# Moving the low halves of the gated products from GpSimd to VectorE, the product copies ahead of weight work on ScalarE, and the token sums and stored x halves of a fused attention and expert kernel

## What is computed

```python
x = x + xattn(layernorm(x), ctx_512, W_k, b_k, ln_gamma, ln_beta)   # softmax over normalised scores
# on layernorm(x):
gate = einsum('btd,edf->ebtf', x, Wg)      # experts 0 and 1: + x Ga Gb
up   = einsum('btd,edf->ebtf', x, Wu)      # experts 0 and 1: + x Ua Ub
mid  = silu(gate) * up
out  = einsum('ebtf,efd->ebtd', mid, Wd)   # experts 0 and 1: + mid Da Db
x = x + einsum('bte,ebtd->btd', weights, out)
```

## Time and profile before

| | us |
|---|---|
| median of 3 runs (range) | 1147.43 (1147.41 to 1148.15) |
| time of the profiled execution | 1149.48 |
| its span, first to last instruction | 1147.8 |
| TensorE busy in the span | 1070.2 (93%) |
| VectorE, ScalarE, GpSimd busy | 776.0, 440.6, 259.8 |

### The profile page before, as it was taken

One profiled execution on the slowest core, in us unless ns is written; L12 is line 12 of the kernel. 1 busy time (PEld: TensorE's weight loads), 2 busy tenths in 40 slices (PEclk: granted clock), 3 DMA queues, 4 the chain that ended last, 5 costly groups with the idle time before them and its releaser, 6 DMA issues.

```text
span 1147.8 us, 12310 instructions
## 1 busy us (share of the span) xinstructions
PE 1070.2 (93%) x4680; PEld 862.9 (75%) x4680; DVE 776.0 (68%) x1155; ACT 440.6 (38%) x634; POOL 259.8 (23%) x184
## 2 busy tenths in 40 slices
PE   6899999688999999999999969899999999999998
PEld 4787777466887878787877758677777878787777
DVE  6788795849486675749485692866757484857743
ACT  3454242343344344434343333443433342534430
POOL 2511144204030221304030210402213040403122
PEclk8899999889999999999999979999999999999999
DMA  8310002253132331414150205102111111211111
GB/s 295 120 46 1 1 15 84 57 176 128 37 116 68 97 105 56 147 55 129 37 181 22 73 18 202 56 19 74 37 56 55 55 38 37 73 36 57 37 38 74
DMA packets 85692, 86.35 MB, mean 75 GB/s; under 512 B 4096, under 2 KB 61568, under 8 KB 84864
## 3 DMA queue, kind: packets, MB, share of 16 engines
q1 hardware_dynamic: 85344, 85.49, 22.9%
q10 hardware_dynamic: 288, 0.07, 0.0%
HBM read 70.86 MB, written 14.68 MB: 75 GB/s over the span
## 4 chain that ended last, share of the span: by engine, by line
PE 55%; DVE 25%; issue 10%; ACT 6%; DMA 3%; SPq 0%; POOL 0%; DVEq 0%; ACTq 0%; POOLq 0%
PE tiles L1361 9%; PE tiles L1363 9%; PE tiles L1362 9%; PE gate_up L1471 6%; PE gate_up L1473 6%; PE gate_up L1472 6%; DVE mids L1131 5%; DVE wd_lo L1093 3%; ACT piece_hi L725 3%; DVE piece_lo L1085 2%; DVE piece L1073 2%; DVE piece L1074 2%; PE gate_up L1430 1%; PE gate_up L1429 1%; PE gate_up L1435 1%
## 5 line engine op out<-in xcount | busy, mean ns | idle before, releaser
L527 POOL TENSOR_TENSOR mids_lo<-mids,mids_hi 128x512 fp32r<-128x512 f32 x112 | 181.5, 1638 | 555.2 <-ACT mids_hi L759 554.6
L1471 PE MATMUL gate_up<-xT_hi,piece_hi 128*128 128x512 f32 x448 | 179.1, 400 | 29.8 <-ACT u_sb L745 28.1
L1085 DVE TENSOR_TENSOR piece_lo<-piece,piece_hi 128x1024 fp32r<-128x1024 f32 x112 | 133.7, 1235 | 106.0 <-ACT piece_hi L725 106.0
L1137 DVE SCALAR_TENSOR_TENSOR xacc<-tiles,rw,xacc 128x512 f32<-128x512 f32 x112 | 78.0, 750 | 163.0 <-PE tiles L1363 163.0
L1361 PE MATMUL tiles<-wd_hi,mids_hi 128*128 128x512 f32 x448 | 176.4, 394 | 9.6 <-POOL mids_lo L527 5.8
L1362 PE MATMUL tiles<-wd_lo,mids_hi 128*128 128x512 f32 x448 | 176.0, 393 | 0.0
L1363 PE MATMUL tiles<-wd_hi,mids_lo 128*128 128x512 f32 x448 | 175.9, 393 | 0.0
L1472 PE MATMUL gate_up<-xT_hi,piece_lo 128*128 128x512 f32 x448 | 175.9, 393 | 0.0
L1473 PE MATMUL gate_up<-xT_lo,piece_hi 128*128 128x512 f32 x448 | 175.4, 391 | 0.0
L1471 PE MATMUL gate_up<-tx_hi,piece_hi 128*128 128x512 f32 x336 | 133.9, 398 | 19.9 <-ACT s_sb L735 16.4
L1472 PE MATMUL gate_up<-tx_hi,piece_lo 128*128 128x512 f32 x336 | 132.3, 394 | 0.0
(11 more groups left out here) (165 smaller groups left out, 1559.6 us busy)
## 6 DMA issues: line engine op xcount, KB each, us to landing
piece<-in_wg_dram SPq DMA_DIRECT2D x40, 256.0 KB, 3.2
piece<-in_wu_dram SPq DMA_DIRECT2D x40, 256.0 KB, 3.3
wd_raw<-in_wd_dram SPq DMA_DIRECT2D x10, 1024.0 KB, 5.1
piece<-merged SPq DMA_DIRECT2D x32, 256.0 KB, 3.3
merged<-lora_w SPq DMA_DIRECT2D x6, 1024.0 KB, 5.3
w_raw<-in_xT_dram SPq DMA_DIRECT2D x4, 1024.0 KB, 6.1
wd_raw<-merged SPq DMA_DIRECT2D x4, 1024.0 KB, 5.6
out_dram<-xacc SPq DMA_DIRECT2D x16, 256.0 KB, 4.5
```

The source lines that it names most:

```text
L527: nc.gpsimd.tensor_tensor(mids_lo[h][:, f, :], mids[h][:, f, :], plain(mids_hi[h][:, f, :]), ALU.subtract)\
L1085: ins = nc.vector.tensor_tensor(piece_lo[j % 3][:, first:last, :], piece[j % 3][:, first:last, :], plain(piece_hi[j % 3][:, first - 1:last ...
L1137: nc.vector.scalar_tensor_tensor(tile_of(b, t), tiles[:, t, :], rw[:, (b * TT + t) * E + s:(b * TT + t) * E + s + 1], tile_of(b, t), ALU.m ...
L1471: nc.tensor.matmul(dst, w_h, x_h, start=first and kt == 0, stop=False, skip_group_check=True)
```

## The change

It moves `mid_low_part`, `lora_b_low_part` and `x_sum` from GpSimd to VectorE; writes VectorE's and ScalarE's orders anew, so that in a regular step the three product copies come before the weight pieces; forms the token sums for steps 0 to 6 between block 3's units; stores x of blocks 2 and 3 as its high and low halves straight from `xT_hi` and `xT_lo` (4 DMAs of 1 MB), loads three of the seven operands of step 7 back in place by six DMAs from GpSimd's queue (`load_again`), and forms the other four in `x_back` during step 6; issues the loads of pieces in step 0 ahead of the wait for the store of `xacc`; and gives the pieces' semaphores one instance per buffer.

```diff
-            sp.wait_ge(x_staged, TT)
-            sp.dma_start(x_spill[0, :, :], zt[:, :, :].rearrange("p t c -> p (t c)")).then_inc(x_stored, 16)
+            def store_x(a):
+                sp.wait_ge(xT_lo_ready, (a + 1) * TT)
+                for part, xT_part in enumerate((xT_hi, xT_lo)):
+                    sp.dma_start(x_spill[a - 2, part, :, :], plain(xT_part[:, a * KT * S:(a + 1) * KT * S])).then_inc(x_stored, 16)
+
+            def quadrant(b, part, first):
+                return x_spill[b, part, :, first * S:(first + 2) * S]
+
+            def load_back(slot, source):
+                sp.dma_start(x_back[:, slot, :], source).then_inc(x_back_loaded, 16)
+
+            store_x(B - 2)
...
+            store_x(B - 1)
...
             sp.dma_start(acc_spill, xacc[:, 2 * TT * D:]).then_inc(acc_stored, 16)
+            load_next_piece(3)
             sp.wait_ge(acc_stored, 16)
-            for k in range(STEPS):
+            load_lora(0)
+            load_next_piece(4)
+            load_next_piece(5)
+            store_merged(0)
+            for k in range(1, STEPS):
...
+                    load_back(0, quadrant(1, 0, 0))
+                    load_back(1, quadrant(1, 1, 0))
+                    load_back(2, quadrant(0, 0, 2))
+                    load_back(3, quadrant(0, 1, 2))
...
-                    sp.wait_ge(x_ready, 11)
+                    sp.wait_ge(x_ready, 8)
                     sp.dma_start(xacc[:, 2 * TT * D:], acc_spill).then_inc(acc_loaded, 16)
                 load_next_piece(4 * k + 3)
+                if k == SWAP - 1:
+                    sp.wait_ge(sums_made, 6)
+                    load_back(1, quadrant(0, 0, 0))
+                    load_back(3, quadrant(0, 1, 0))
+                    sp.dma_start(x21_spill, x_back[:, 2, :]).then_inc(x21_stored, 16)
...
+            def load_again(b, first, product):
+                pool.wait_ge(p_mm[product], 4 * SWAP)
+                cols = slice((b * KT + first) * S, (b * KT + first + 2) * S)
+                for part, xT_part in enumerate((xT_hi, xT_lo)):
+                    pool.dma_start(xT_part[:, cols], x_spill[b, part, :, first * S:(first + 2) * S].bitcast(f32r)).then_inc(x_again[product], 16)
...
-            pool.wait_ge(x2_ready, B * TT)
-            stage(B - 2)
-            pool.wait_ge(xT_lo_ready, B * TT)
-            pool.wait_ge(x_stored, 16)
-            stage(B - 1)
-            low_part(B - 1, 0)
-            low_part(B - 1, 1)
-
...
-            for k in range(STEPS):
-                if k < len(LORA_JOBS):
-                    lora_b_low_part(k)
-                for m in range(2):
-                    for c in (C12, C11, C22, C21):
-                        mid_low_part(k, m, c)
+            for f in range(FT):
+                low_part(B - 1, f)
+            pool.wait_ge(x_stored, 64)
+            load_again(0, 0, 1)
+            load_again(1, 2, 3)
+            load_again(0, 2, 2)
...
+                    piece_high_part(j + 3)
+                    if lora:
+                        lora_high_parts(k)
                 else:
-                    gate_silu(k, 0, C21)
+                    mid_high_part(k - 1, 1, C12)
+                    copy_p1(j)
+                    mid_high_part(k - 1, 1, C11)
+                    copy_p5(j)
+                    mid_high_part(k - 1, 1, C22)
+                    copy_u2(j)
+                    mid_high_part(k - 1, 1, C21)
+                    piece_high_part(j + 1)
+                    for c in (C12, C11, C22, C21):
+                        gate_silu(k, 0, c)
+                    piece_high_part(j + 2)
...
                     copy_p1(j + 2)
                     copy_p5(j + 2)
+                    copy_u2(j + 2)
                     piece_high_part(j + 4)
-                    copy_u2(j + 2)
-                wd_high_part(k)
+                    wd_high_part(k)
                 for c in (C12, C11, C22):
                     mid_high_part(k, 0, c)
                 copy_p1(j + 3)
                 copy_p5(j + 3)
+                copy_u2(j + 3)
+                mid_high_part(k, 0, C21)
                 if k in (0, SWAP):
                     piece_high_part(j + 4)
...
+            def mid_low_part(k, m, c):
+                dve.wait_ge(mids_hi_made, 8 * k + 4 * m + c + 1)
+                h, f = 1 if c in (C12, C22) else 0, m if c in (C12, C11) else m + 2
+                nc.vector.tensor_tensor(mids_lo[h][:, f, :], mids[h][:, f, :], plain(mids_hi[h][:, f, :]), ALU.subtract)\
+                  .then_inc(mids_lo_made, 1)
...
+            dve.wait_ge(sim_mm, B * TT)
+            x_sum(0, 1, 0)
+            x_sum(1, 0, 0)
+            dve.wait_ge(sums_made, 2)
+            difference(tx_sum[:, 1, :], tx_sum[:, 0, :], tx_sum[:, 1, :])
             unit(B - 1, 0)
             read_logitsT(B - 1, tiles)
+            dve.wait_ge(transposed, B * TT)
+            x_sum(2, 1, 2)
+            dve.wait_ge(sums_made, 3)
+            difference(t3_sum[:, :], tx_sum[:, 2, :], tx_sum[:, 0, :])
             unit(B - 1, 1)
+            dve.wait_ge(t_made, 2)
+            difference(tx_sum[:, 2, :], tx_sum[:, 2, :], tx_sum[:, 1, :])
             read_logits(B - 1, tiles)
+            x_sum(0, 0, 2)
             router(B - 1)
             unit(B - 1, 2)
-            piece_sums(0)
-            dve.wait_ge(sums_made, 2)
-            difference(tx_sum[:, 1, :], tx_sum[:, 0, :], tx_sum[:, 1, :])
...
             dve.wait_ge(sums_made, 4)
             dve.wait_ge(t_made, 3)
             difference(tx_sum[:, 0, :], tx_sum[:, 0, :], tx_sum[:, 2, :])
-            t_low_part(3, 6)
-            t_low_part(2, 7)
-            t_low_part(4, 4)
+            piece_sums(0)
+            t_low_part(1, tx_lo[:, 1, :], tx_sum[:, 1, :], tx_hi[:, 1, :])
+            unit(B - 1, 3)
+            t_low_part(3, tx_lo[:, 2, :], tx_sum[:, 2, :], tx_hi[:, 2, :])
+            t_low_part(2, xT_lo[:, t3], t3_sum[:, :], xT_hi[:, t3])
+            t_low_part(4, tx_lo[:, 0, :], tx_sum[:, 0, :], tx_hi[:, 0, :])
+            piece_low_part(0)
             piece_sums(1)
+            piece_low_part(1)
...
+                    dve.wait_ge(x_back_loaded, 16 * 9)
+                    dve.wait_ge(t_made, 7)
+                    difference(x_back[:, 2, :], x_back[:, 2, :], x_back[:, 3, :])
+                    mid_low_part(k - 1, 1, C22)
+                    make_mid(k - 1, 1, C21)
+                    t_low_part(5, tx_lo[:, 1, :], x_back[:, 1, :], tx_hi[:, 1, :])
+                    t_low_part(6, tx_lo[:, 2, :], x_back[:, 3, :], tx_hi[:, 2, :])
+                    mid_low_part(k - 1, 1, C21)
+                    t_low_part(7, xT_lo[:, t3], x_back[:, 0, :], xT_hi[:, t3])
                     piece_sums(j + 1)
...
+                    t_low_part(8, tx_lo[:, 0, :], x_back[:, 2, :], tx_hi[:, 0, :])
+                    piece_low_part(j + 1)
+                    add_down(k - 1, 0)
+                    add_down(k - 1, 1)
...
                 make_mid(k, 0, C12)
                 combine(k, UP, 0, C22)
                 make_mid(k, 0, C11)
+                mid_low_part(k, 0, C12)
                 make_mid(k, 0, C22)
-                if k < len(LORA_JOBS):
-                    add_lora(k)
-                wd_low_part(k)
+                mid_low_part(k, 0, C11)
                 if k in (0, SWAP):
+                    if lora:
+                        add_lora(k)
+                    mid_low_part(k, 0, C22)
                     piece_sums(j + 4)
-                make_mid(k, 0, C21)
-                if k in (0, SWAP):
+                    make_mid(k, 0, C21)
                     piece_low_part(j + 4)
+                else:
+                    piece_low_part(j + 4)
+                    mid_low_part(k, 0, C22)
+                    wd_low_part(k)
+                    if lora:
+                        add_lora(k)
+                    make_mid(k, 0, C21)
                 combine(k, UP, 1, C12)
+                mid_low_part(k, 0, C21)
                 combine(k, UP, 1, C11)
                 make_mid(k, 1, C12)
...
-                    pe.wait_ge(x_ready, 5)
+                    pe.wait_ge(x_again[1], 32)
```

## The result

The changed kernel took 1088.1 (median; 1086.62 to 1088.33, 4 runs) against 1147.42 for the one before on the same chip: a ratio of 0.9479, 95% interval 0.9463 to 0.9495. That is 59.3 won. The forecast was 1078.5, with 1071 to 1098 as its range: the median lies inside, 9.6 above the forecast. The profiled execution took 1088.33 with a span of 1086.6, against 1149.48 and 1147.8.

A forecast was written before the change was run, and what follows sets the result against it. TensorE, busy 1070.2 of 1147.8, was taken as the bound, so only its waits could be won: 1.4 + 16.1 + 10 + 14.3 + 4 + 23 = 68.8 off the median 1147.43 gave 1078.6, forecast as 1078.5, range 1071 to 1098.

The forecast's parts named there:

- Block 3: Before step 0: staging on GpSimd goes and the last unit's product comes earlier; 1.4 won.
- Step 0: Step 0 takes 46.7 in place of 62.8, with waits of 8.1 left; 16.1 won.
- Steps 1 to 5: Regular steps with low rank: waits of about 2 a step shrink to 0.3 at P4; 10 won with step 1's extra.
- The exchange: Step 6 and the halves ahead of step 7: waits and slow matmuls go, one wait of 3.3 remains; 14.3 won.
- The clock holds: At the second half ahead of step 7: no fall to half clock after the 3.3 wait, as after 3.13 idle before.
- The exchange is late: Rival, 11%: in step 6 loads, sums and stored halves share DMA queues and run late by 10 to 20; 1088 to 1098.
- the prediction's own signs of being wrong: P1, P4 or P6 waiting on VectorE every step, clock 0.5 at the exchange, or TensorE waiting for stored halves.
- Step 7: Step 7 keeps 2 of its 6 of waits; 4 won.
- Steps 8 to 13: Regular steps without low rank: all waits, 3.5 a step, go, and 2 more for step 8; 23 won.
- the leak in each step: Rival, 21%: VectorE runs 1.5 to 2 behind in each regular step, 18 to 24 back over 12 steps; 1100.
- the six loads on GpSimd's queue: 512 KB loads with 34 from release in quad 3 to first use; cost taken as 0, bounds 0 and over 100.
- each VectorE instruction so met costs 1.1 more: VectorE beside GpSimd: a surcharge of 1.1 per instruction, on at least four at a step's end and as many in quad 0.

The follow-up runs named there:

- Experiment 10: The changed kernel with the load of piece 3 in step 0 issued behind the xacc store wait and first low-rank loads, as before: 1091.19.
- experiment 3: The changed kernel with the next piece's sums ahead of the merge and its halves ahead of the C21 product's, in steps 0 and 7: 1084.15.
- Experiments 1 and 2: The changed kernel with step 7's first additions ahead of piece sums, last split and piece: 1082.05; or with two stored-half loads ahead of a piece load: 1085.02.
- experiment 7: The kernel before with ScalarE's copies first in quads 0 and 3 of every step, low halves still on GpSimd: 1147.88.
- experiment 6: The changed kernel with ScalarE's copies of quads 0 and 3 back in their old places, low halves still on VectorE: 1132.51.
- experiment 5: The changed kernel with all 112 low halves of the gated products back on GpSimd, every other order as changed: 1105.8.
- Experiment 9: The kernel before with copies first in quads 0 and 3, and VectorE's next-piece low half behind quad 0's three combinations: 1119.14.
- experiment 8: The kernel before with copies first in quads 0 and 3, and ScalarE's next-piece high half ahead of the C21 product's in quad 0: 1147.28.

## Why the prediction was right, and where not

The steps' lengths are read from TensorE's starts, before and after.

| stage | before | changed | won | forecast |
|---|---|---|---|---|
| start of step 0 | 210.98 | 209.52 | 1.5 | 1.4 |
| step 0 | 62.8 | 46.7 | 16.1 | 16.1 |
| steps 1 to 5 | 320.2 | 311.8 | 8.3 | 10 |
| step 6 with both halves | 101.2 | 93.2 | 8.0 | 14.3 |
| step 7 | 43.2 | 39.2 | 4.0 | 4 |
| steps 8 to 13 | 382.3 | 359.7 | 22.6 | 23 |

- **Block 3.** Forecast 1.4 and a first matmul at 209.5; measured 1.46 and 209.52. That it fits so closely is luck: in the traces of the experiments, which change nothing ahead of step 0, that matmul starts between 208.5 and 209.8 for the changed order and between 209.7 and 211.9 for the old one.
- **Step 0.** Forecast 46.7 long, 16.1 won; measured 46.7 (209.52 to 256.2). The waits are the named ones: low-rank 2.23 idle at 240.11 where 239.9 was worked out, the last one 3.01 ahead of the next P1, on `piece_lo`. Experiment 10 bears out that the low-rank matmuls hang on the order of SyncE's queue.
- **Steps 1 to 5.** Forecast 10, measured 8.3. Steps 2 to 5 are 62.1, with 0.28 at P4 where 0.3 was forecast. The rest is mostly step 1: the wait of 3.01 ahead of it was foreseen, the nine matmuls or so at half clock behind it were not. In experiment 3 the wait is 1.02 and the slow matmuls are gone.
- **The exchange.** This is the step of the prediction that failed: 14.3 forecast, 8.0 measured. Its chain for VectorE started from an engine that is on time at the end of step 6. It was not: two stored halves landed late, VectorE stood 8.20, and P6 waited 2.48, with its slow matmuls 4.2 in all. The second half started 3.7 late where 3.3 was worked out, and the sentence "The clock holds" was wrong: it fell to half, which added 1.7. These three, 4.2, 0.4 and 1.7, are the 6.3 that are missing here. Experiments 1 and 2 show each of the two waits alone. The lateness of the stored halves is the mechanism of the rival "The exchange is late" (11%), through the place of a load in SyncE's queue, and the time of 1088.1 lies where the forecast's own range ends and that rival's begins (1088). Two of the prediction's own signs of being wrong came true: clock 0.5 at the exchange, and a wait of TensorE that goes back to the stored halves.
- **Step 7.** Forecast 4, measured 4.0.
- **Steps 8 to 13.** Forecast 23, measured 22.6; 59.9 a step as forecast (60.3 in step 8), with no wait inside them.

The sum is 60.6 against 68.8; of the 8.2 that are missing 6.3 are the exchange, 1.7 steps 1 to 5 and 0.4 steps 8 to 13. The medians differ by 59.3 and not by 60.6, mainly since the profiled execution of the kernel before was 2.1 above its median and that of the changed kernel 0.2. Nothing of the leak in each step (the largest rival) appeared, and the six loads on GpSimd's queue cost nothing: they landed 4.6 and 6.0 after issue (medians), and TensorE never waits for them.

The prediction named two causes of the waits, GpSimd beside VectorE and the copies' place, and added their removal up in one sum. The experiments show that they can't be added. The kernel before is at 1148.0 (in the runs beside these). The copies of quads 0 and 3 first, alone, give 1147.9 (experiment 7), everything but these copies 1132.5 (experiment 6), everything but the low halves 1105.8 (experiment 5), and all of it 1088.1. Experiment 9 reaches 1119.1 with these copies first and one piece moved on VectorE. So the right order on the two engines is worth about 29 with the surcharges in place, and the low halves' move 17.7 on top of the changed order. No run moves the low halves alone, so what they are worth with the old order is not known; nor did a run take apart block 3, or step 0 beyond the one load of experiment 10. The statement that "each VectorE instruction so met costs 1.1 more" holds in size (1.10 in experiments 5, 7 and 8), but it is met once per GpSimd instruction. The prediction's rows had that already: over the four VectorE instructions of the earlier trace rows, 1.1 and 2.2 more than alone make three surcharges, for the three subtractions of the earlier trace rows, where the prediction counted "at least four instructions". And about half of it falls where VectorE has time to spare; so experiment 5 cost 17.7 where its expectation had some 30. That did not touch the forecast itself, whose regular step was counted from waits.

Open is what decides between full and half clock after a wait; the last section has what the traces show of it. The forecast took one row, 3.13 idle without a fall, as a rule for a wait of 3.3, though in the earlier trace rows the clock fell after 3.85.

## What to carry to other kernels

A wait that ends at one copy hides the next lateness behind it: before an edit is priced, follow the engine that releases the wait past that point and look for the second wait (P4 here) that comes out when the first is gone. In strict queues place work by when it is wanted: a piece that TensorE needs in 12 belongs behind a combination that it needs in 2, and a load that nothing can go on without ahead of a load that waits for a buffer. An elementwise job on GpSimd is only worth having where no VectorE instruction with two SBUF inputs runs beside it; here eight of 0.60 cost VectorE 7.7 when they ran on GpSimd and 4.8 when VectorE did them itself. And a forecast that adds up waits should carry a term for the clock behind the longer ones: here it was nothing or 1.0 to 2.8, and the shortest wait with a fall behind it was 1.81 idle (experiment 7).

## What the runs showed of the hardware

- A GpSimd subtraction makes a VectorE instruction with two SBUF inputs beside it longer by up to 1.10, whatever the size of the latter: 128x256 takes 1.51 for 0.41, a pair of 128x512 2.38 for 1.28, 128x1024 and 128x768 together 3.19 for 2.09. A product that starts 0.49 or 0.38 after the subtraction takes less, 0.66 more (862.57 in experiment 7, 1.34 long) or 0.79 more (895.25 in experiment 5, 1.47 long). A combination that reads one input from PSUM takes none: 0.69 at 928.95 before, beside a subtraction from 928.51. The Trainium skill (SBUF — State Buffer, Who interferes with whom) has the second instruction wait out the first. The trace agrees with that better than the prediction thought. A subtraction that meets no such instruction takes 1.28 to 1.30 (928.51 before, 871.91 in experiment 7), and the two products above are held until about 1.16 after the subtraction's start (1.34 - 0.68 + 0.49 and 1.47 - 0.68 + 0.38, an estimate from these rows). The mean of 1.84 in the earlier trace rows, against which the prediction set the 1.1, contains GpSimd's own waiting: behind VectorE's `piece_lo` a subtraction takes 1.81 (872.13 in experiment 8).
- The granted clock after a wait does not follow from the length of the idle time, nor from the place of the wait in the kernel. The same wait at P6 of quad 3 in step 6, 2.48 idle, is followed by six matmuls or so at half clock in the changed kernel (625.62, shown above) and by none in experiment 10:

```profile
628.93 0.50 PE L1516 MATMUL gate_up<-tx_hi,piece_hi 128*128 128x512 f32 x1 [2.48 <-ACT s_sb L735]
629.26 0.40 PE L1517 MATMUL gate_up<-tx_hi,piece_lo 128*128 128x512 f32 x1
```

Ahead of the second half the clock fell after 3.56 (648.57) and held after 3.44 in experiment 3 (645.62); at P4 of quad 0 in experiment 8 it held after 1.83 in step 9 (813.61) and fell after 1.83 in step 10 (876.61), both steps alike in their work; before, it held after 3.13 (736.15). At half clock (1.2 in place of 2.4 GHz) matmuls start 0.43 apart in place of 0.227, and a fall cost 1.7 at 648.57 and 1.4 at 625.62. What decides is not shown by these runs.
